# A hand-over threshold of 3 raised to 6 in the attention loop of a transformer layer on eight cores

## The reference, cut to what matters

```python
xn = _layernorm(x, axis=-1)
# attention
k = jnp.einsum('ihd,bpd->biph', W_K, xn)
q = jnp.einsum('ihd,bpd->biph', W_Q, xn)
v = jnp.einsum('ihd,bpd->biph', W_V, xn)
scores = jnp.einsum('biph,biqh->biqp', k, q)
scores_masked = jnp.tril(scores) - 10000000000.0 * (1.0 - mask)
attn = jax.nn.softmax(scores_masked / np.sqrt(d_head), axis=-1)
z = jnp.einsum('biph,biqp->biqh', v, attn)
out_a = jnp.einsum('df,bqf->bqd', W_O, z_flat)
# experts
sel = jax.nn.sigmoid(jnp.einsum('bsd,ed->bse', xn, expert_sel))
h = jax.nn.relu(jnp.einsum('bsd,edh->bseh', xn, keys))
out_f = jnp.einsum('bseh,ehv,bse->bsv', h, values, sel)
return x + out_a + out_f
```

## Time and profile before

| what | us |
| --- | --- |
| median of the 2 timed runs | 10549.14 |
| the 2 timed runs | 10463.94 and 10634.33 |
| the profiled execution, its own time | 10211.51 |
| its span, core 6, first to last instruction | 10209.4 |
| the spans of its 8 cores | 10130.8 to 10209.4 |
| granted TensorE clock of its cores, mean | 0.824 to 0.830 |

### The profile page before, as it was taken

One profiled execution on the slowest core, in us unless ns is written; L12 is line 12 of the kernel. 1 busy time (PEld: TensorE's weight loads), 2 busy tenths in 40 slices (PEclk: granted clock), 3 DMA queues, 4 the chain that ended last, 5 costly groups with the idle time before them and its releaser, 6 DMA issues.

```text
span 10209.4 us, 85985 instructions; the slowest of 8 cores (10130.8 to 10209.4 us)
## 1 busy us (share of the span) xinstructions
PE 7533.0 (74%) x19968; PEld 3369.3 (33%) x19968; DVE 1493.0 (15%) x3384; ACT 1630.1 (16%) x4009; POOL 80.1 (1%) x164
## 2 busy tenths in 40 slices
PE   4767789987666767788946666798777666667898
PEld 2323333333333333333422222343333333333333
DVE  2111110001111111110021111101011111111100
ACT  2111210002222222210021111100022222222000
POOL 0000000000000000000000000000000000000000
PEclk7766777778888888899977777799888888888999
DMA  1000012220000000012220000022200000000122
GB/s 46 7 13 13 7 34 63 61 54 1 7 7 7 7 7 7 1 38 78 66 62 7 13 7 13 16 67 75 53 7 1 7 7 7 7 7 1 52 74 73
DMA packets 552181, 274.49 MB, mean 27 GB/s; under 512 B 211520, under 2 KB 539456, under 8 KB 551744
## 3 DMA queue, kind: packets, MB, share of 16 engines
q1 hardware_dynamic: 543040, 251.95, 9.6%
q0 software_dynamic: 8704, 17.05, 0.4%
HBM read 251.92 MB, written 16.78 MB: 26 GB/s over the span
## 4 chain that ended last, share of the span: by engine, by line
PE 68%; issue 11%; DVE 8%; ACT 6%; DMA 3%; SPq 2%; DVEq 1%; ACTq 1%; POOLq 0%; POOL 0%
PE psZ L554 13%; PE psA L679 10%; PE psB L730 9%; PE psA L360 7%; PE psT L573 7%; PE psB L378 7%; PE psB L722 5%; PE psA L414 5%; ACT pool L489 3%; PE psA L452 3%; DVE pool L530 3%; SPq L186 2%; ACT pool L192 2%; PE psT L660 1%; DMA pool<-wv 1%
## 5 line engine op out<-in xcount | busy, mean ns | idle before, releaser
L554 PE MATMUL psZ<-pool 128*128 128x512 f32 x2304 | 1418.8, 702 | 446.3 <-DVE pool L195 150.9
L452 PE MATMUL psA<-pool 64*128 64x512 f32 (+3 forms) x1280 | 849.6, 767 | 973.1 <-ACT pool L489 677.5
L573 PE MATMUL psT<-ident_sb,pool 128*128 128x128 f32 x4608 | 845.4, 321 | 455.9 <-DVE pool L530 347.7
L573 PEld LDWEIGHTS psT<-ident_sb,pool 128*128 128x128 f32 x4608 | 694.5, 169 | 1196.7 <-issue 1196.6
L679 PE MATMUL psA<-xn,pool 128*128 128x512 f32 x2048 | 980.2, 635 | 1.8 <-PE psT L660 1.8
L730 PE MATMUL psB<-pool 128*128 128x512 f32 x2048 | 938.7, 619 | 0.0
L360 PE MATMUL psA<-xn,pool 128*128 128x512 f32 x1536 | 768.9, 659 | 170.5 <-issue 79.7
L457 PE MATMUL psB<-pool 64*128 64x512 f32 (+3 forms) x1280 | 864.2, 779 | 0.0
L452 PEld LDWEIGHTS psA<-pool 64*128 64x128 f32 x1280 | 259.2, 244 | 1517.8 <-issue 1517.7
L192 ACT ACTIVATE pool<-psT 128x512 f32<-128x512 f32 x672 | 401.5, 597 | 2177.4 <-PE psT L573 1856.3
L378 PE MATMUL psB<-xn,pool 128*128 128x512 f32 x1536 | 694.9, 607 | 0.0
(11 more groups left out here) (56 smaller groups left out, 3271.8 us busy)
## 6 DMA issues: line engine op xcount, KB each, us to landing
pool<-keys SPq DMA_DIRECT2D x128, 512.0 KB, 3.9
pool<-vals SPq DMA_DIRECT2D x64, 1024.0 KB, 7.0
pool<-x SPq DMA_DIRECT2D x64, 512.0 KB, 3.8
pool<-wo SPq DMA_DIRECT2D x64, 512.0 KB, 4.0
pool<-wq SPq DMA_DIRECT2D x64, 256.0 KB, 3.8
pool<-wk SPq DMA_DIRECT2D x64, 256.0 KB, 4.9
pool<-wv SPq DMA_DIRECT2D x64, 256.0 KB, 5.0
out<-pool POOLq DMA_DIRECT2D x32, 512.0 KB, 4.6
```

Source lines behind the costliest of these rows:

```text
L452: (eng.matmul(psA[jb][:, 0:w], qS[0:64, cc * 128:cc * 128 + 128], kS[0:64, j * 512:j * 512 + w], start=True, stop=True, tile_position=(0, 0)),
L554: eng.matmul(psZ[sb_z][:, :], vT[:, i * 128:(i + 1) * 128], EnT[:, tb * 512: (tb + 1) * 512], start=(i == 0), stop=(i == n_i - 1)),
L573: r2 = eng.transpose(psT[tb][:, col:col + 128], En[:, slot + i * 128: slot + i * 128 + 128], ident[:, :])
```

## The change

The threshold on `lead` goes from 3 to 6. The counter, its start at 0, the condition on "EXPS" and the closing loops are as before.

```diff
@@ -617,7 +617,7 @@
                                 tz = None
                             elif tz is not None:
                                 lead += 1
-                                if lead > 3:
+                                if lead > 6:
                                     next(tz, None)
                         if tz is not None:
                             for _ in tz:
```

## The result

| what | kernel before | changed kernel |
| --- | --- | --- |
| timed runs of the first measurement | 10 | 11 |
| median, us | 10568.3 | 10603.7 |
| lowest and highest, us | 10259.4, 10848.8 | 10002.1, 11025.1 |
| ratio over the runs taken as comparable | | 0.9479 (95% interval 0.9383 to 0.9574) |

The two medians lie 0.3% apart, and the ratio says 5% faster. The ratio leaves out executions in which a die ran at a visibly lower granted clock than the other, or that lay far above the fastest of their kernel. What was left of the changed kernel are four executions at 10,002 to 10,016 us. The record does not say what they were divided by. Worked back from the ratio it is 10006/0.9479 = 10,556 us, near the median of the ten times of the kernel before, 10,568. So it seems that the shortest executions of one kernel were set against ordinary ones of the other.

The account below looks back on a forecast made before the run. TensorE was taken to bound the kernel, with 1875 us idle in the attention loop. Nothing added, removed or moved (0 us), so the forecast stayed at the median before, 10549 us, range 10172 to 10673.

Parts of the forecast that it names:

- The change, step by step: Hand-overs in the attention loop: `lead` stays at most 1, instruction lists identical; 96 hand-overs x 0 steps = 0 us.
- Within 2%: Whole kernel: the time after stays within 2% of the median before, 10549 us; chance 0.92.
- rival C: Same program, comparison still differs since executions fall elsewhere; faster by 2% (10338 us or less) 0.05, slower 0.03.
- The price of the clock: Dense lines' matmuls: all at 703 ns cost 597 us more (10809), all at 592 ns 183 us less (10029).
- the dense lines: Projections, experts and output (lines 360, 378, 414, 679, 722, 730): 4342 us of TensorE busy time, hardly any idle.
- A: Attention-loop hand-overs: threshold bites, weighting steps move uncovered into the closing loop; 187 to 362 us slower; with B 0.01.
- B: Attention-loop hand-overs: threshold bites, fewer copies stand ahead of exponentials on ScalarE; 43 us faster; with A 0.01.

Follow-up runs that it names:

- threshold 0: Threshold 0 in place of 3 on the kernel before, same program byte for byte: 10,227 ± 8 us at clock 0.82, measured median 10,437 us.
- drawn by pieces: Against the kernel before, each "EXPS" draws only the weighting slices its exponentials overwrite, not all; with threshold 3: 10,007 ± 6 us at clock 0.82.
- the two matmuls held back: Against drawn by pieces with threshold 3: copies drawn with their transposes, last two weighting matmuls after the next pair's scoring steps; 9836 ± 6 us at clock 0.82.
- threshold 6: In the hardware section: threshold 6 in place of 3 on the kernel drawn by pieces, 10,131 ± 8 us at clock 0.82.
- no draw by the counter: Threshold 1000, never reached, on the kernel drawn by pieces; only the EXPS rule and closing loop draw; 10,167 ± 6 us at clock 0.82.

## Why the prediction was right or wrong

**The change, step by step: right.** `lead` never passes 1, the two programs are equal byte for byte, and the sum of 0 us holds to +5 ± 7 us. The block of ten slices behind one score step stood where it was expected, and so did the counts and the busy times of VectorE and ScalarE. The run with threshold 0 shows the same from the other side.

**The forecast against the measured ratio: wrong.** "Within 2%" had 0.92, and the measurement said 5% faster. This is rival C on its fast side, with 0.05. The step that failed is the one that priced C. It took the three executions at hand as the spread of the program, with 10,211 us as the fast end, and so the range began at 10,172, although its own price of the clock went down to 10,029. The program does 9983 to 10,019 us on undisturbed dies. It also said, with nothing measured behind it, that a comparison made in alternation would take most of the difference away. The runs showed that such a comparison can miss by 5% with equal programs. For the kernel before 14 of 80 die points were at the high clock, and an execution is short only with both dies there, which 2 of its 40 executions were. Of the twelve executions of the changed kernel recorded in the first measurement four were. The ten of the kernel before seem to have had none (their lowest is 10,259); their clocks are not recorded, so this is concluded from their times and not seen. That the four fell to the changed kernel was luck as far as the program goes; what decides on the clock of a die stays open.

**The price of the clock: right in kind, too small in size.** The prediction gave the dense lines 597 us at most, and so took 10,809 us as the far end. Dies were measured up to 11,084 us, at a clock of 0.724. (Its 253 us between the profiled execution and the shorter timed run are 252, which changes nothing.) The dense lines are not alone: in the profile of after they account for 446 us of the 636 that TensorE's busy time grew by. Most of the rest is in the loop (line 554 from 1418.8 to 1511.7 us, line 452 from 849.6 to 894.3). Over all dies of the kernel before the price is 89 us for 0.01 of mean granted clock. The profiled executions, at 0.827 and 0.763 on the cores shown, should differ by 568 us by it and differ by 574. The rule of the Trainium skill that the prediction cited (TensorE: Matmul & The Clock Gate, the note on the peak-current limiter) has the whole die at 13/16 of the clock once three of its cores run dense matmuls, for as long as they do. The dense stretches at 0.81 agree with the fraction. The measurement speaks against the rest: in the profiled execution of the kernel before, all four cores of die 0 were busy for the whole 80 us from 4420 to 4500 us, with a granted clock of 1.00. Each core's time counts from its own first instruction, so that this holds only as far as the four began together.

**Rivals A and B: did not occur, and are now priced.** Where the threshold bites, A had 187 to 362 us of loss and B 43 us of gain. Measured on the kernel in which it bites: 124 ± 10 us slower, at equal clock. The sign is A's, with a third of the size that I took. The mechanism that shows is another: not steps left uncovered at the end, but copies that slipped behind the row scaling on VectorE, with 108.5 us of waits put down to it. How much of the 124 us that makes is open.

**The time.** The predicted 10,549 us stands 0.5% below the measured median of 10,604, but that nearness means little, since medians of this one program came out between 10,369 and 10,678.

## What to carry to other kernels

Before pricing a constant in scheduling code, follow the values that are compared with it; a block of work in the timeline that the constant should have cut shows in a minute that it is dead. A ratio of 0.95 with a narrow interval is not proof of a faster program: compare the programs, and compare times at equal granted clock, by die. And where such a threshold is alive, as in the kernel drawn by pieces, do not price it by the number of steps that it delays; ask which of them then fall behind a long operation in the list of another engine.

## What the runs showed of the hardware

The median granted clock of the four cores of a die ranged from 0.724 to 0.848 for one unchanged program, in executions of the same job on the same chip, and the span followed it along a straight line with a scatter of about 20 us, 0.2%. I had not expected one number to explain so much.

The highest clock that a die showed differed between kernels: 0.8485 for the kernel before, 0.8615 when drawn by pieces with threshold 3, 0.8795 with the two matmuls held back. Of the difference on the dies with the highest clock (9990 to 9362 us, 6.3%), only 394 us (3.9%) remain at equal clock; the rest came with the clock. That shorter waits of TensorE keep the clock up is one reading, and it is not shown. In these three kernels the idle time before the three lines falls as that clock rises (1875, 1650, 1440 us), but threshold 6 with 1716 us showed 0.8485 at most in 12 points, and no draw by the counter, with more idle time, 1777 us, showed 0.8585. No run varied the waits alone.
